# Eight more causal masks per batch on GpSimd, three edits to the order of ACT, POOL and DVE, and v of two steps on VectorE

## The reference

```python
qkv = layernorm(x) @ W_qkv
scores = einsum('bhqd,bhkd->bhqk', q, k) / 8 + slope[h] * (kpos - qpos)
scores = where(qpos >= kpos, scores, -inf)
x = x + (softmax(scores) @ v) @ W_out
H = gelu(((layernorm(x) @ U1) @ V1) + b1)
x = x + (H @ U2) @ V2 + b2
```

## Time and profile before

| | us |
|---|---|
| median of three runs | 2753.2 |
| profiled execution, its own time | 2755.6 |
| its span, first to last instruction | 2753.5 |
| PE busy | 2638.1 (96%) |
| POOL busy | 2170.1 (79%) |
| ACT busy | 2160.9 (78%) |
| DVE busy | 1999.5 (73%) |

### The profile page before, as it was taken

The page is one execution under the profiler, slowest core; times in us unless marked ns, Lnnn a source line. Parts: engine busy times, 40 slices in busy tenths (PEclk is TensorE's granted clock), DMA queues, the critical chain, the costliest instruction groups (busy, mean ns, idle before and its releaser), DMA issues.

```text
span 2753.5 us, 83206 instructions
## 1 busy us (share of the span) xinstructions
PE 2638.1 (96%) x30344; PEld 1793.8 (65%) x30344; DVE 1999.5 (73%) x6825; ACT 2160.9 (78%) x3888; POOL 2170.1 (79%) x2221
## 2 busy tenths in 40 slices
PE   5999999999999999999999999999999999999985
PEld 2666666666666666666666666667666666666663
DVE  5678777776777777777776777778677786776753
ACT  4877878878788887878878788887878878887882
POOL 4878778787877878788787887878788787887884
PEclk8999999999999999999999999999999999999997
DMA  6444444444445445444444444444444444544421
GB/s 181 99 97 96 93 97 93 97 94 92 98 89 105 92 90 102 93 96 97 95 95 91 98 91 99 95 93 95 93 103 91 91 101 90 100 93 95 97 49 31
DMA packets 489111, 260.74 MB, mean 95 GB/s; under 512 B 310064, under 2 KB 485168, under 8 KB 488704
## 3 DMA queue, kind: packets, MB, share of 16 engines
q1 hardware_dynamic: 488704, 255.44, 44.9%
HBM read 27.73 MB, written 8.39 MB: 13 GB/s over the span
## 4 chain that ended last, share of the span: by engine, by line
PE 71%; ACT 9%; issue 8%; POOL 7%; DMA 3%; DVE 2%; SPq 1%; ACTq 0%; POOLq 0%; DVEq 0%
PE proj L540 34%; PE scores L540 17%; PE o_acc L540 12%; PE max_scores L540 8%; POOL p_lo L1264 4%; ACT p_hi L808 2%; ACT p_f L858 2%; ACT L858 2%; ACT h_f L953 2%; POOL h_lo L1296 2%; DMA o_t<-o_hi_lo 1%; DMA q_operands<-neg_max_t_lo 1%; PE proj L702 1%; DVE xn_t_lo L979 0%; POOL o_hi_lo L1278 0%
## 5 line engine op out<-in xcount | busy, mean ns | idle before, releaser
L1264 POOL TENSOR_TENSOR p_lo<-p_f,p_hi 128x512 f16<-128x512 f32 x1280 | 1483.9, 1169 | 372.8 <-ACT p_hi L808 372.0
L1038 DVE CUSTOM_DVE_ANT_0 max_scores<-max_scores,causal 128x512 f32<-128x512 f32 (+3 forms) x2048 | 971.1, 506 | 399.3 <-PE max_scores L540 359.9
L808 ACT ACTIVATE p_hi<-p_f 128x512 f16<-128x512 f32 x1280 | 800.6, 625 | 93.4 <-POOL p_f L1258 84.1
L858 ACT ACTIVATE p_f<-scores 128x512 f32<-128x512 f32 x1280 | 752.8, 588 | 151.4 <-PE scores L540 124.3
L540 PE MATMUL scores<-q_operands,k_lo_hi 128*128 128x512 f16 (+3 forms) x2048 | 607.2, 300 | 23.7 <-ACT p_f L858 17.2
L540 PE MATMUL scores<-q_operands,k_hi_aug 128*128 128x512 f16 (+3 forms) x2048 | 564.9, 299 | 0.0
L540 PE MATMUL o_acc<-v_hi_one,p_lo 128*128 128x65 f16 x5120 | 518.1, 194 | 34.4 <-POOL p_lo L1264 33.6
L540 PE MATMUL o_acc<-v_hi_one,p_hi 128*128 128x65 f16 x5120 | 517.7, 194 | 0.0
L540 PE MATMUL o_acc<-v_lo,p_hi 128*128 128x64 f16 x5120 | 517.1, 193 | 0.0
L540 PEld LDWEIGHTS o_acc<-v_hi_one,p_lo 128*128 128x128 f16 x5120 | 470.9, 98 | 68.9 <-POOL p_lo L1264 48.2
L540 PE MATMUL max_scores<-k_hi_aug,q_operands 96*128 96x512 f16 (+3 forms) x2048 | 491.8, 302 | 12.0 <-DMA k_lo_hi<-k_pair_lo 8.5
(11 more groups left out here) (133 smaller groups left out, 4392.5 us busy)
## 6 DMA issues: line engine op xcount, KB each, us to landing
q_operands<-q_pair_hi SPq DMA_DIRECT2D x512, 128.0 KB, 2.5
q_operands<-q_pair_lo SPq DMA_DIRECT2D x512, 64.0 KB, 2.1
k_hi_aug<-k_pair_hi SPq DMA_DIRECT2D x256, 64.0 KB, 2.0
k_lo_hi<-k_pair_hi SPq DMA_DIRECT2D x256, 64.0 KB, 2.0
k_lo_hi<-k_pair_lo SPq DMA_DIRECT2D x256, 64.0 KB, 2.0
x_rows<-in_L_attn_inputs SPq DMA_DIRECT2D x17, 512.0 KB, 4.3
x_acc<-in_L_attn_inputs SPq DMA_DIRECT2D x64, 128.0 KB, 2.4
out<-x_rows SPq DMA_DIRECT2D x16, 512.0 KB, 3.2
```

Of the source, the lines that this page charges most:

```text
L808: return nc.scalar.activation(out_ap, in_ap, ACT.Copy, scale=scale)
L858: nc.scalar.activation(p_f[:, n, :], score_bank[(SEG * s + n) % 2][:, :], ACT.Exp).then_inc(exp_done, 1)
L1038: last = nc.vector.tensor_tensor_reduce(out=bank, in0=bank, in1=causal[:, (T - 1 - qt) * P:S], scale=1.0, scalar=-3e38, op0=ALU.add, op1=A ...
L1264: nc.gpsimd.tensor_tensor(p_lo[:, place, :], p_f[:, n, :], p_hi[:, place, :], ALU.subtract).then_inc(lo_p, 1)
```

## The change

1. Masks: `POOL_MASKS` gets eight more segments per batch: (6,2), (6,3), (12,2), (14,2), (14,3), (15,2), (15,3), (15,4). In them PE no longer adds the mask (two matmuls fewer in each), POOL selects.
2. Attention's high half (`hi_o` on ACT) goes from segment 4 to segment 0 of the next step, behind `high_p` and `exponentiate` there (`O_LAG`).
3. `pp` (high on ACT, low on DVE) goes one segment later (`PP_LAG`).
4. Of the two `h_lo` on POOL the second goes three segments later (`ODD_LAG`).
5. v of steps 0 and 2: the high half goes from ACT in segment 0 of the next step to DVE at the end of segment 4 (`high_v`), with the low half behind it.
6. DVE's order: `k_pair_lo` goes ahead of the maxima of its segment, and the transposed x of (15,3) and (15,4) (`X_PAIRS`) behind `normalise`.

```diff
-MASK_STEPS = (0, 2, 4, 5, 8, 9, 10, 11)
-POOL_MASKS = [(s, n) for s in MASK_STEPS for n in range(2, SEG)]
+MASK_STEPS = {0: (2, 3, 4), 2: (2, 3, 4), 4: (2, 3, 4), 5: (2, 3, 4), 6: (2, 3), 8: (2, 3, 4), 9: (2, 3, 4),
+              10: (2, 3, 4), 11: (2, 3, 4), 12: (2,), 14: (2, 3), 15: (2, 3, 4)}
+POOL_MASKS = [(s, n) for s, blocks in MASK_STEPS.items() for n in blocks]
...
-V_LAG = 1
+V_LAG, O_LAG, PP_LAG, ODD_LAG = 1, 1, 1, 3
+
+DVE_V = (0, 2)
+ACT_V = [s for s in range(KV) if s % 8 < 4 and s not in DVE_V]
...
+                        so, segment = before(s, n, O_LAG)
+                        if segment == O_SEG and in_stage(mode, s, ATT + 2):
...
+                            act.wait_ge(o_done, at(2 * (a + 1)))
+                            copy(o_hl[:, slot, 0, :], o_f[:, slot, :, :].rearrange("p t c -> p (t c)")).then_inc(hi_o, 1)
...
-                        if n == O_SEG and in_stage(mode, s, ATT + 1):
...
+                def high_v(s):
+                    t = s % 8
+                    dve.wait_ge(pe_v, at(i * 8 + t + 1))
+                    if 2 * (i * KV - 8) > 0:
+                        dve.wait_ge(pe_av, at(2 * (i * KV - 8)))
+                    nc.vector.tensor_scalar(v_hi[:, t, 0:8, 0:HD], proj("v", s)[:, :].rearrange("p (k d) -> p k d", d=HD),
+                                            KV_OUT, None, ALU.mult).then_inc(hi_v_dve, 1)
...
+                        if n == K_SEG + k_lag(s) and s % 2 == 1 and mode in (FIRST, MID):
+                            dve.wait_ge(hi_k, at(i * (KV // 2) + (s + 1) // 2))
+                            low(ks[1][:, :], proj("k", s)[:, :], ks[0][:, :], KV_OUT).then_inc(lo_k, 1)
                         if in_stage(mode, s, 2):
                             maxima(s, n)
...
+                        if n == V_SEG and s in DVE_V and mode in (FIRST, MID):
+                            high_v(s)
+                            dve.wait_ge(hi_v_dve, at(i * len(DVE_V) + DVE_V.index(s) + 1))
+                            low_v(s)
...
                         if (s, n) in split_pairs(i, s):
-                            f, pair = ffn_batch(i, s), split_pairs(i, s)[s, n]
-                            for c in (2 * pair, 2 * pair + 1):
...
+                            low_h(ffn_batch(i, s), 2 * split_pairs(i, s)[s, n])
+                        so, segment = before(s, n, ODD_LAG)
+                        j = i if so >= 0 else i - 1
+                        if (so % KV, segment) in split_pairs(j, so % KV):
+                            low_h(ffn_batch(j, so % KV), 2 * split_pairs(j, so % KV)[so % KV, segment] + 1)
```

More of the change, by code:

```diff
@@ L900, in body @@
                             high_p(s - 1, SEG - 1)
+                        if before(s, n, PP_LAG) in U1_AT and mode != FIRST:
+                            t = U1_AT[before(s, n, PP_LAG)]
+                            act.wait_ge(pe_pp, at((i - 1) * 4 + t + 1 + FREE))
+                            if t == 0:
+                                act.wait_ge(pe_h, at((i - 1) * FC + FREE))
+                            copy(pp[0:RANK, t * P:(t + 1) * P], proj("p", t)[0:RANK, 0:P], 1.0 / FFN_SCALE).then_inc(hi_pp, 1)
                         if in_stage(mode, s, ATT):
@@ L903, in body @@
                         sv, segment = before(s, n, V_LAG)
-                        if segment == V_SEG and sv % 8 < 4 and mode in (FIRST, MID):
+                        if segment == V_SEG and sv in ACT_V and mode in (FIRST, MID):
                             t, half = sv % 8, sv // 8
@@ L1070, in statistics, with low_v @@
                     nc.vector.tensor_scalar(veps2[:, t:t + 1], agg2[:, t, 1:2], EPS, None, ALU.add).then_inc(ve2, 1)
+                def low_v(s):
+                    t, half = s % 8, s // 8
+                    heads = slice(half * 8, (half + 1) * 8)
+                    low(v_lo[:, t, heads, :], proj("v", s)[:, :].rearrange("p (k d) -> p k d", d=HD),
+                        v_hi[:, t, heads, 0:HD], KV_OUT).then_inc(lo_v, 1)
+                def high_v(s):
[5 more added lines that the diff above has]
+                                            KV_OUT, None, ALU.mult).then_inc(hi_v_dve, 1)
                 def normalise(s, h):
@@ L1105, in body @@
                         sv, segment = before(s, n, V_LAG)
[L1106 to L1111, removed]
-                        if n == K_SEG + k_lag(s) and s % 2 == 1 and mode in (FIRST, MID):
-                            dve.wait_ge(hi_k, at(i * (KV // 2) + (s + 1) // 2))
-                            low(ks[1][:, :], proj("k", s)[:, :], ks[0][:, :], KV_OUT).then_inc(lo_k, 1)
+                        if segment == V_SEG and sv in ACT_V and mode in (FIRST, MID):
+                            dve.wait_ge(hi_v, at(i * len(ACT_V) + ACT_V.index(sv) + 1))
+                            low_v(sv)
                         if n == q_segment(s) + q_lag(s) and mode in (FIRST, MID):
@@ L1169, in body @@
                             normalise(s, n // 2)
+                        if (s, n) in X_PAIRS and mode in (FIRST, MID):
+                            pair = X_PAIRS[s, n]
+                            if pair == 0:
+                                dve.wait_ge(pe_q, at((i + 1) * KV))
+                            dve.wait_ge(pe_ln1, at(2 * (i + 1) + pair + 1))
+                            nc.vector.tensor_copy(xnt[0][:, :, pair * 256:(pair + 1) * 256],
+                                                  proj("x", pair)[:, :].rearrange("p (c q) -> p c q", c=DC)).then_inc(hi_ln1, 1)
+                            low_x(i + 1, pair)
                         if (s, n) in u2_pairs(i, s):
```

51 lines of the change are left out of this document (19 added, 32 removed).

## The result

| | median us | runs | against before |
|---|---|---|---|
| before | 2754.0 | 4 (2751.1 to 2755.6) | |
| after | 2791.1 | 4 (2780.3 to 2792.8) | 1.0129 [1.0111, 1.0147] |

The change makes the kernel 37 us slower; 8 were forecast, with a range up to 2773. The profiled execution of after took 2792.5 us (span 2790.5, 37.0 more than before). The page's first part answers to the earlier trace rows: TensorE is busy 5 us longer with 256 matmuls fewer, so something made its matmuls longer.

The account below looks back on a forecast made before the run. PE, busy 96%, was taken as the bound, held by four kinds of stop. +21.0 + 0.8 - 8.4 - 5.1 = +8.3 on the profiled 2755.6 gave 2763.9, forecast as a median of 2761; range 2740 to 2773.

Parts of the forecast that it names:

- The chain of (0,1): Step 15 into (0,1): selects delay POOL's `p_lo`, attend starts 1.4 us later, fifteen times, 21.0 us.
- the 3.6 us for VectorE's casts: Moved `p_lo` and selects on POOL: contention with VectorE would cost 0.24 per batch, 3.6 us; not counted in the forecast.
- lies under: In (0,1), the scores' wait for the exponentiation of (15,4), until 1142.92, falls within the later attend's delay.
- The second low half: Second `h_lo` of (13,2) leaves POOL ahead of (14,1): attend's 0.34 us stop there goes, 5.1 us saved over fifteen batches.
- 0 to 0.3 us: `o_hi_lo` one segment later delays POOL's low half and the transposing DMA by this much (1.2 in (1,0)).
- The last pass: POOL is the bound there; the selects of (6,2) and (6,3) add 0.38 each, 0.8 us.
- The masks saved: PE loses two 0.056 us matmuls per new segment; five of eight segments kept, 0.56 per batch, 8.4 us in all.
- The rest at nothing: `k_pair_lo` ahead of the maxima, v on DVE, `pp` and `X_PAIRS` were each forecast to change nothing in time.
- rival 2: No change: ACT's chain ends sooner without the `k_pair_lo` stop, up to 9 us kept, 2752; chance 0.14.
- Rival 1: Faster: POOL's load decides, not its order; the stop of (0,1) stays, the gains remain, 2740; chance 0.18.
- which the masks make idle: `X_PAIRS` behind `normalise` frees ACT of its 0.54 us wait for DVE, worth nothing with the selects in.
- Rival 3: Slower: the select's wait spreads, one more PE stop of 0.8 us per batch, 12 us, 2773; chance 0.15.

Follow-up runs that it names:

- filler: The changed kernel with twelve unused 250-column matmuls added on PE in (0,1), ahead of its wait for `p_lo`: 2772.0 us, ratio 1.006.
- control: The kernel before with the same twelve unused matmuls in (0,1): 2751.9 us, ratio 0.9994.
- e1_no15: The changed kernel without its three selects in step 15, PE adding those masks again: 2732.0 us, ratio 0.9917.
- e12: e1_no15 with the gelus' second low half behind the first again in steps 1 and 3 alone: 2722.5 us, ratio 0.9882.
- e15: e12 with `X_PAIRS` (VectorE's casts of the next batch's x) ahead of `normalise` again in (15,3) and (15,4): 2722.0 us, ratio 0.9886.
- e14: e12 with POOL's selection also in (6,4), (12,3) and (14,4), six mask matmuls fewer per batch: 2730.5 us, ratio 0.9913.
- e13: e12 with v of steps 0 and 2 on ScalarE again, VectorE doing its low half alone: 2726.2 us, ratio 0.9898.
- e9: e1_no15 with the high half of attention's output one segment earlier again (`O_LAG` 0 in place of 1): 2727.6 us, ratio 0.9900.

## Why the prediction was wrong

**The chain of (0,1): right.** 7.0 us were forecast and measured in all batches with gelus. Fourteen of the fifteen times stand in the table's step 0 (19.4), the fifteenth in the last pass (1.2): 20.6 for 21.0. The first `p_lo` behind the gelus took 1.16 us, as counted (POOL's timeline, 1153.48), so the 3.6 us for VectorE's casts beside it didn't come.

**The price of the stop in (0,1): wrong, and the largest part.** The step that failed is "attend starts at 1145.65 instead of 1144.24: 1.4 us later ... fifteen times: 21.0". It priced the stop as time that passes and took TensorE's speed behind it as given. The prediction even named both halves of the new pattern, the scores' wait until 1142.92 and the longer one for `p_lo`, and said the first "lies under" the second. In time it does. For the clock it doesn't: PE was busy 1.25 of 3.9 us there, and the clock fell. The filler and its control show 19.1 us of the 28.7 that the forecast lacked to be that.

**The second low half: right in (14,1), wrong in (5,1).** The stop of (14,1) is gone (step 14 0.54 shorter, forecast 0.56). But only that place was worked out. The same edit puts an `h_lo` on POOL into (4,0), ahead of the selects and `p_lo` that attend of (5,1) waits for; with `o_hi_lo` coming later too, that costs 5.4 us. The prediction gave the later `o_hi_lo` "0 to 0.3 us" and looked at transposes and out projections only, not at what stands behind it on POOL.

**The last pass: direction right, size wrong** (6.2 for 0.8; 1.2 of it are the chain of (0,1), as said, which leaves 5.0). There PE has little to do, and ACT and POOL set the pace [windows above: step 1 of the last pass 11.65 for 9.59, ACT busy 10.90 of it]. Each of three edits undone (both `h_lo` together, `o_hi_lo` earlier, the old masks) takes 2.4 to 2.8 us off e1_no15's 122.6. But e12 and e15, which run the same instructions in that stretch, measured 119.9 and 118.4, and before with and without the filler, which isn't in the last pass, 116.1 and 118.4: single profiles scatter there by 1.5 to 2.2, nearly as much as each of the three effects. No single cause is shown.

**The masks saved: the unit right, the sum half right.** In (14,3) the row pairs of before and of after stand 0.22 and 0.17 us apart, the mask matmul of 0.056 gone from between them.

```profile
1125.20 0.33 PE L540 MATMUL scores<-q_operands,k_lo_hi 128*128 128x384 f16 x1
...
1125.42 0.32 PE L540 MATMUL scores<-q_operands,k_hi_aug 128*128 128x384 f16 x1
```

```profile
1139.18 0.33 PE L546 MATMUL scores<-q_operands,k_lo_hi 128*128 128x384 f16 x1
1139.35 0.32 PE L546 MATMUL scores<-q_operands,k_hi_aug 128*128 128x384 f16 x1
```

Segment (14,3) went from 2.532 to 2.420 us, 0.112 for two, as carried; the Trainium skill's sustained spacing of about 81 ns ("TensorE: Matmul & The Clock Gate", Back-to-back issue gap) would have made it 0.162, and the trace does not agree. Step 15's savings are swallowed (11.40 us in both), as forecast. Step 12 gave nothing: its segment (12,2) is 0.11 shorter, but PE's wait for attention's transposes in (12,4) grew by 2.2 us in sum. Step 6 gave nearly twice the forecast, since the waits for the transposed maxima in (7,0) shrank with it, by 2.8 us, and e14 shows that this can turn: three more segments saved, 8 us lost.

**The rest at nothing: right.** Without `k_pair_lo` in the way the waits of (13,4), (1,4) and (3,4), on average of the batches, grew from 0.49, 0.42 and 0.45 to 0.65, 0.58 and 0.59 and took the saving whole, so rival 2 gave nothing. `X_PAIRS` does nothing measurable; v left alone the waits that the prediction named for it, and whether the 3.7 us of e13 are its doing stays open.

**Rival 1** (POOL's load, not its order) was wrong as stated, with all three selects in. Without them the order is worth far more than I carried: attend at 4.97 even with both `h_lo` in place, where before had 5.62. 0.37 of that 0.65 is POOL's wait for ACT's `p_hi` of (15,4), gone once `o_hi_lo` stands behind that `p_hi`: with `o_hi_lo` put back alone (e9) the wait is there again, 0.36, and with `X_PAIRS` put back alone (e15) attend stays at 4.59. Another 0.24 is the first `p_lo`, 1.16 us for 1.40; it took 1.16 in every kernel with the changed order, and no run shows which edit does it. The prediction counted the 0.54 of the earlier trace rows to `X_PAIRS`, "which the masks make idle", and the later `o_hi_lo` as a delay alone: with the masks in, the gain can't be seen, and that is why taking those of step 15 back out was the best move.

**Rival 3** (12 us more through one more stop per batch) was the right kind of error at the wrong place: the stop was in (5,1), and what pushed the time past its 2773 was the clock.

## What to carry to other kernels

Price a stop of TensorE twice: once as the time it takes, and once by what the granted clock does behind it, since the second cost comes in steps and not in proportion: here none up to 1.85 us, and with 0.1 us more a fall at every second stop. Where an in-order engine gets an instruction that can start only after a late producer, count everything queued behind it, at every place where the edit puts one, not only where it was meant to help. A saved matmul was worth its spacing here only where TensorE didn't wait for a transfer behind it.

## What the runs showed of the hardware

TensorE's granted clock fell to its lower level for 3.4 us (once 6.8) in or close behind stops of 1.93 us and more from start to start (22 of 33), and in or behind none of 1.30 to 1.85 us (55), though PE was busy 159.2 of the 162.9 us between two of the low stretches (993.11 to 1156.00 in after). Two like batches of one kernel differed in it. Twelve unused matmuls in the stop of (0,1) kept the clock at 1.00 through step 0 of all fourteen batches with that stop, worth 19.1 us of 2791. Chains over ACT and POOL came out alike from batch to batch: in after attend stood 6.99 to 7.00 us behind the exponentiation in all fourteen. A `p_lo` of 128x512 on POOL took 1.16 us, a select of 128x256 0.41.
